# Moving the last group's routing pieces ahead among the first expert tiles, and narrowing the memsets between its row scatters

## The reference

```python
x = x + tanh(g_xattn) * xattn(ctx, layernorm(x), mask, mask, ...)
xn = layernorm(x)
scores = sigmoid(xn @ gate.T + bias)            # 2048 tokens x 9 experts
top_scores, selected = top_k(scores, 2)         # divided by their sum
for e in range(9):
    h = silu(xn @ w1[e].T) * (xn @ w3[e].T)     # hidden size 352
    out = out + cw[:, e:e+1] * (h @ w2[e].T)
x = x + tanh(g_ffn) * out
```

## Time and profile before

| what | us |
|---|---|
| median of 3 runs (lowest, highest) | 239.15 (238.38, 239.47) |
| the profiled execution's own time | 237.12 |
| its span in the trace | 235.3 |
| PE busy | 196.8 |
| DVE, ACT, POOL busy | 141.3, 142.6, 131.9 |

### The profile page before, as it was taken

The page is one execution under the profiler, slowest core; times in us unless marked ns, Lnnn a source line. Parts: engine busy times, 40 slices in busy tenths (PEclk is TensorE's granted clock), DMA queues, the critical chain, the costliest instruction groups (busy, mean ns, idle before and its releaser), DMA issues.

```text
span 235.3 us, 5763 instructions
## 1 busy us (share of the span) xinstructions
PE 196.8 (84%) x1527; PEld 156.2 (66%) x1528; DVE 141.3 (60%) x511; ACT 142.6 (61%) x400; POOL 131.9 (56%) x229
## 2 busy tenths in 40 slices
PE   8999986999999998997796799907999999999100
PEld 3676754666667665664685789807899999998100
DVE  1469996788997698887394794401344433443045
ACT  2287859988878786886258456602666666665100
POOL 4246844233325876776878587777555555655400
PEclk9999999999999999999799999985999999999855
DMA  6999999999300100011471321113221122160095
GB/s 182 352 380 250 405 382 363 400 326 292 117 4 13 37 23 23 25 35 38 101 225 38 91 51 55 45 34 98 64 67 43 54 54 61 46 215 27 0 329 206
DMA packets 19546, 32.65 MB, mean 139 GB/s; under 512 B 2609, under 2 KB 11830, under 8 KB 19394
## 3 DMA queue, kind: packets, MB, share of 16 engines
q1 hardware_dynamic: 16498, 27.18, 35.9%
q0 software_dynamic: 2304, 4.24, 5.5%
q10 hardware_dynamic: 720, 0.95, 1.4%
HBM read 15.77 MB, written 17.10 MB: 140 GB/s over the span
## 4 chain that ended last, share of the span: by engine, by line
PE 54%; DVE 16%; POOL 8%; issue 8%; ACT 8%; DMA 4%; SPq 0%; POOLq 0%; DVEq 0%; ACTq 0%
PE pt_ps L1230 9%; PE score_ps L1192 5%; PE score_ps L1194 4%; PE score_ps L1193 4%; PE pt_ps L1239 4%; PE score_ps L1050 4%; PE ps_a L1100 3%; POOL x_rows L564 3%; PE pt_ps L1088 3%; PE pt_ps L990 3%; ACT probs L385 3%; DVE xs L982 3%; PE score_ps L1000 2%; PE ps_b L1157 2%; POOL spare L550 2%
## 5 line engine op out<-in xcount | busy, mean ns | idle before, releaser
L582 POOL DMA_INDIRECT y_rows<-probsT,ids x40 | 39.6, 990 | 25.2 <-ACT probsT L453 17.2
L385 ACT ACTIVATE probs<-score_ps,less 128x128 f32<-128x128 f32 x128 | 37.8, 418 | 0.4 <-DVE less L773 0.4
L924 DVE TENSOR_TENSOR xg_low<-ps_a,xg_high 128x128 fp32r<-128x128 f32 x40 | 11.7, 292 | 43.5 <-ACT xg_high L438 26.8
L564 POOL DMA_INDIRECT x_rows<-stage,slot x32 | 32.5, 1017 | 8.0 <-POOL spare L550 4.5
L1230 PE MATMUL pt_ps<-w,probsT 128*128 x234 | 33.4, 280 | 2.1 <-ACT probsT L460 2.1
L1230 PEld LDWEIGHTS pt_ps<-w,probsT 128*128 128x128 f32 x234 | 31.3, 194 | 3.2 <-issue 2.9
L453 ACT ACTIVATE probsT<-pt_ps,xg 128x128 f32<-128x128 f32 x39 | 14.3, 367 | 30.0 <-PE pt_ps L1230 23.5
L1192 PE MATMUL score_ps<-w_high,xg_low 128*128 x80 | 30.3, 379 | 0.6 <-DVE probs L931 0.2
L931 DVE TENSOR_TENSOR probs<-probs,score_ps 128x352 f32<-128x352 f32 x40 | 20.8, 520 | 12.2 <-issue 6.1
L1193 PE MATMUL score_ps<-w_low,xg_high 128*128 x80 | 26.4, 330 | 0.0
L1194 PE MATMUL score_ps<-w_high,xg_high 128*128 x80 | 26.3, 328 | 0.0
(11 more groups left out here) (153 smaller groups left out, 427.6 us busy)
## 6 DMA issues: line engine op xcount, KB each, us to landing
x_rows<-pads SPq DMA_DIRECT2D x1, 9945.0 KB, 39.5
w_low<-in_w13T SPq DMA_DIRECT2D x3, 1056.0 KB, 10.8
xg<-x_rows SPq DMA_DIRECT2D x40, 65.0 KB
ctx_r<-in_ctxT SPq DMA_DIRECT2D x4, 512.0 KB, 7.2
w<-in_w2T SPq DMA_DIRECT2D x1, 1728.0 KB, 13.4
kheads<-y_rows SPq DMA_DIRECT2D x3, 512.0 KB, 5.0
mask_b<-in_mask SPq DMA_DIRECT2D x4, 256.0 KB, 7.9
out<-xs SPq DMA_DIRECT2D x1, 1024.0 KB
```

What stands on the lines that cost most here:

```text
L385: last = nc.scalar.activation(probs[:, r % 2, h, :], score_ps[:, r % 2, h, :], ACT.Exp, bias=less[:, r % 2, h:h + 1])
L564: pool.indirect_dma_start(x_rows[:, :], bass.IndirectOffsetOnAxis(ap=slot[:, par, c, p:p + 1], axis=0), stage[:, par, c, p, :], None, boun ...
L582: pool.indirect_dma_start(y_rows[:, :], bass.IndirectOffsetOnAxis(ap=ids[:, r:r + 1], axis=0), yt[:, r, :], None, bounds_check=last_row, o ...
```

## The change

The pieces that the last group needs before its rows can be scattered stand one to two tiles earlier, and some pieces change place with them:

- Batch 15's row transposes (`turn_rows(18)` on PE, `turned_back(18)` on ACT) go into tile 3: on PE behind the six products with w1 and w3 and ahead of the products with w2; on ACT behind the silu and ahead of the scaling.
- `gate_and_out(18)` on PE and the two table loads with the exponential on ACT go from behind tile 4 to behind tile 3.
- On DVE `table_counts(1)` goes from tile 2 to tile 0; logits and clamp from 4 to 3; `table_rows(1)` stays in 3 but behind them; `make_keys(3)` from 5 to 3; `choose(3)` from 6 to 4; weigh, ranks, places and labels from 7 to 5; `table_used(1)` and `table_counts(2)` from 8 to 6; `table_rows(2)` from 9 to 7. `rank(3)` on PE goes from 7 to 5.
- On POOL the scatters of the last group stand behind the y scatters of tiles 1, 1, 2 and 3 instead of 3, 4, 5 and 6. The memsets of the last group are 128x128 instead of 128x384 and the one behind each scatter is gone. Group 2 keeps its own.

```diff
@@ scalar: tile, between
+                if isinstance(k, int) and k == 3:
+                    turned_back(NB + 2)
...
                 if k == 3:
-                    turned_back(NB + 2)
-                if k == 4:
                     nc.scalar.preload_act_table(ACT.Exp)
                     sigmoid_exps(NG - 1)
                     nc.scalar.preload_act_table(ACT.Silu)
@@ gpsimd
-            def space():
+            def space(n):
-                nc.gpsimd.memset(spare[:], 0.0).then_inc(spaced, 1)
+                nc.gpsimd.memset(spare[:, 0:n], 0.0).then_inc(spaced, 1)
...
-                        space()
+                        space(3 * D if g < NG - 1 else D)
...
                 tile(k, k % TR)
-                if k in range(3, 3 + UN):
-                    scatter(NG - 1, k - 3)
-                    space()
+                for p in {1: (0, 1), 2: (2,), 3: (3,)}.get(k, ()):
+                    scatter(NG - 1, p)
@@ vector: between
                 if k == 0:
                     norm2(NB - 2)
                     table_used(0)
+                    table_counts(1)
                 if k == 1:
                     second(NB - 1)
                 if k == 2:
-                    table_counts(1)
                     norm2(NB - 1)
                 if k == 3:
-                    table_rows(1)
-                if k == 4:
                     logits_of(NG - 1)
                     clamp(NG - 1)
+                    table_rows(1)
+                    make_keys(NG - 1)
+                if k == 4:
+                    choose(NG - 1)
                 if k == 5:
-                    make_keys(NG - 1)
-                if k == 6:
-                    choose(NG - 1)
-                if k == 7:
                     weigh(NG - 1)
                     keep_ranks(NG - 1)
                     place_rows(NG - 1)
                     label_rows(NG - 1)
-                if k == 8:
+                if k == 6:
                     table_used(1)
                     table_counts(2)
-                if k == 9:
+                if k == 7:
                     table_rows(2)
@@ tensor: tile, between
+                if isinstance(k, int) and k == 3:
+                    turn_rows(NB + 2)
...
                 if k == 3:
-                    turn_rows(NB + 2)
-                if k == 4:
                     gate_and_out(NB + 2)
-                if k == 7:
+                if k == 5:
                     rank(NG - 1)
```

## The result

The changed kernel took 237.3 us (median of 20 runs, 235.27 to 239.56). The kernel before took 239.47 (20 runs, 237.57 to 240.4). The ratio is 0.9908, with a 95% interval of 0.9884 to 0.9931. The gain is 2.2 us where 10.8 were predicted, and the time lies outside the predicted range. The profiled execution took 237.52 with a span of 235.7; before, the two were 237.12 and 235.3.

A forecast was written before the change was run, and what follows sets the result against it. PE, busy 84% of the span, was taken to set the pace. Tile 16 starting 8.6 us earlier plus 2.2 from full clock made 10.8, so 239.15 us became 228.4, range 225.5 to 232.5.

The forecast's parts named there:

- PE's own arrival: PE's path through the early expert tiles to tile 16, forecast at 151.4 us, later than its data at 149.7.
- T(16): Start of PE's transpose of tile 16, other tiles likewise; forecast 8.6 us earlier, at 151.4 instead of 160.02.
- the 0.3 allowed for entering the loop: Allowance of 0.3 us added to seven even tiles, taking PE's transpose of tile 16 from 151.1 to 151.4.
- ACT's gap of 2.58: ACT's unexplained 2.58 us wait ahead of 134.24; might delay data to 151.6, no change to the sum.
- B: Rival: tile 16's data still come last, at 154.4; time 231.4 to 233.5 us; chance 0.13.
- C: Rival: DVE's routing pieces hold up PE's early tiles; 236.4 us in full, 231 if half; chance 0.12.
- costed at 0.2 each: DVE's 16 small operations from logits to keys, estimated at 3.2 us together, ending at 124.7.
- The row transfer of 1.42: POOL's time per last-group transfer with its narrowed memset, forecast at 1.42 us instead of 1.65.
- D: Rival: no measurable change, because the labels come when they did before; 239 us; chance 0.03.
- E: Rival: slower, as DVE's work holds up POOL's descriptor writing and stretches its transfers; 241.5 us; chance 0.02.
- theory S: Theory from the experiments, not the prediction: POOL's indirect transfers standing too close together make PE's releases reach ACT and DVE late.
- 2.2 for the clock: Tile 16 on PE, forecast 2.2 us shorter because without idle time ahead it runs at full clock.

The follow-up runs named there:

- r1: The changed kernel without any edit, run again on the fourth chip; 226.21 us, ratio 0.9525 to the kernel before.
- e8: The changed kernel with the last group's memsets 128x256 instead of 128x128; 227.83 us, ratio 0.9617.
- r3: The kernel before in its old order, with only the last group's memsets narrowed to 128x128 and none behind its scatters; 234.34 us, ratio 0.9845.
- e1 to e4: First chip: changed kernel with 128x384 last-group memsets; plus those behind scatters; old order, narrow memsets; first variant plus early y-scatter memsets: 236.76, 237.69, 237.87, 239.24 us.
- e5: The changed kernel with 128x384 last-group memsets and a 128x128 memset ahead of the y scatters of tiles 4 to 36; 227.27 us, then 227.2.

## Why the prediction went wrong, point by point

**The step that failed** is PE's own arrival: "From there on nothing stands between tiles: seven tiles at 2.06 to 2.07". On the chip of the result four of these tiles took 17.3 us where four at 2.07 take 8.3. That is 9.0 of the 11.8 by which T(16) missed its 151.4. In place of the even pace stood late releases of ACT and DVE and the low clock behind them. Of the rest, 3.0 was already there at T(9), 139.6 against 136.6. The two add up to some 0.3 too much, because the 0.3 allowed for entering the loop wasn't needed.

**Its sign was in the trace before.** ACT's gap of 2.58 has no named releaser either. The prediction put it at nothing in its sum and counted it once in rivals B and C. It wasn't the only one. DVE's timeline of the kernel before has another:

```profile
167.09 0.52 DVE L931 TENSOR_TENSOR probs<-probs,score_ps 128x352 f32<-128x352 f32 x1 [1.60 <-remote]
```

As one of a kind that can come back at every tile, it would have had to stand in the range as often as tiles lie open. The prediction leaned there on the Trainium skill (Runtime: NRT & Kernel Launch, Instruction fetch mechanics) for a gap at a place of the stream. The trace disagrees: r1 has the same streams and not one such gap, and in the late execution the longest came at one instruction, L456, of four tiles in a row.

**The 3.0 us up to T(9)** are partly DVE's. Its counts, logits, clamps and table rows were costed at 0.2 each. In the changed kernel on the chip of the result (DVE's timeline) some took 0.64 to 0.76:

```profile
115.66 0.68 DVE L874 TENSOR_SCALAR in_tiles<-placed 1x9 f32<-1x9 f32 x1
...
123.39 0.68 DVE L702 TENSOR_SCALAR logits<-z 128x36 f32<-128x36 f32 x1
...
125.13 0.64 DVE L894 TENSOR_SCALAR row_of<-row_f 1x8 int32<-1x8 f32 x1
...
126.91 0.76 DVE L713 TENSOR_SCALAR over<-sigs 128x36 f32<-128x36 f32 x1
```
```profile
115.35 0.97 POOL L565 DMA_INDIRECT x_rows<-stage,slot  x1 [0.28 <-POOL spare L551]
...
123.09 0.97 POOL L565 DMA_INDIRECT x_rows<-stage,slot  x1 [0.28 <-POOL spare L551]
...
124.76 0.97 POOL L565 DMA_INDIRECT x_rows<-stage,slot  x1 [0.28 <-POOL spare L551]
...
126.68 0.99 POOL L565 DMA_INDIRECT x_rows<-stage,slot  x1 [0.28 <-POOL spare L551]
```

The second fence is POOL's timeline. Each DVE operation ends within 0.04 us of the transfer that POOL is issuing: 115.66 + 0.68 is 116.34, and 115.35 + 0.97 is 116.32. In r1 the four took 0.57, 0.18, 0.16 and 0.30, 1.55 us less together, and from logits to keys DVE needed 3.2 there (122.34 to 125.52), as forecast. This isn't the mark of a late chip: in e8, with no late release, L702, L894 and L713 took 0.65, 0.63 and 0.76. Labels ended at 133.71 here, 131.13 in r1 (forecast 130.1).

**Point by point where nothing is late (r1)**, forecast ahead of measured: T(5) 125.3 and 126.34; POOL's first memset 130.8 and 131.76; T(9) 136.6 and 137.20; last row scatter 144.2 and 145.53; T(16) 151.4 and 152.36; T(17) behind it 2.1 and 2.11; no wait ahead of T(16); clock around it near 1 and 1.00. The row transfer of 1.42 is 1.47 (133.23 less 131.76, memset to memset). The times up to T(16) are 0.6 to 1.3 us late. T(39) comes at 201.02, before at 211.87: 10.85 sooner, where 10.8 was forecast. That the two agree so well is luck. T(16) came 7.66 sooner, not 8.6, and tile 16 gave 2.12. The remaining 1.07 came behind T(17), where the forecast had nothing (47.62 us from T(17) to T(39) before, 46.55 in r1): the trace of before has its second unnamed wait there. r3 prices the memsets alone: 3.2 us of the whole (237.55 less 234.34).

**The rivals.** B fell: none of the three traces of the changed kernel shows PE waiting for data at T(16). C named the right place, tile distances of 3 us and more, but not the releaser: DVE's pieces weren't it. D fell: the labels did come sooner, at 133.71 and 131.13 instead of 135.36. E said the opposite of what came: the last group's transfers kept their 0.97 to 1.00, and it was DVE whose operations grew longer beside POOL's. E's 241.5 doesn't follow from its own sum either: ten transfers longer by twice 1.15 would put T(16) 11.5 later still, near 252. What came had no rival of its own: the gap of the earlier trace rows, recurring.

**What stays open.** What differs where releases were late (in the runs of the result and on the first chip) isn't known. There the kernel before took 239.5 and 239.8, on the other four chips 236.3 to 237.6. The kernel before loses 2 to 3.5 us there, the changed kernel 11; their traces have two and nine unnamed waits of over 0.5 us.

Late releases are tied in time to POOL's transfers, and more closely than theory S asked. In the six traces with late releases (before, after, e1 to e4) ACT and DVE start 49 times behind a wait without a named releaser from 110 to 180 us. Each of these starts lies 0.62 to 0.82 or 1.33 to 1.51 us behind the start of one of POOL's indirect transfers, while starts behind named waits lie at any distance. Above, 145.30 is 0.71 and 146.01 is 1.42 behind 144.59. All waits of over 0.5 us among them stand in or just behind stretches of transfers at 1.50 or less; row transfers at 1.68 have none. In the other 14 traces no such wait occurs, with transfers as close as 1.27. So spacing seems to decide where releases are late on a chip that has them, and something else whether it has them. The test of the first half would be e5 on a late chip, and e5, run twice, never met one. Why releases come late, and whether some counter or queue is shared with POOL's transfers, no run shows.

**A better version?** None was found. Where nothing is late the changed kernel takes 226.2 and 226.7, its variants with the new order 226.4 to 227.8; none is below it by what the runs can tell. For a chip with late releases it stays open.

## What to carry to other kernels

An idle gap whose releaser has no name is a term of its own: look how often its kind could recur in the work that the change exposes, and keep that in the range. Before a difference of a few per cent is explained by the kernel, run the unchanged kernel on a second chip; four experiments on one chip agreed on a cause that four other chips didn't show. Where nothing else stood in the way, a stall taken away by moving work forward paid nearly what its rows said (7.66 of 8.6 us at T(16), 2.12 of 2.2 for the clock).

## What the runs showed of the hardware

**A release can be 2 us late on one chip and in time on the next.** PE's product ended at 139.35, and ACT, idle, started at 141.58. In this stretch ACT's late starts fell on steps of about 0.74 us (141.58, 142.31, 143.78, 146.01, 146.74, 148.23) and DVE's on the same steps (140.84, 145.30, 149.74), half of the 1.48 between POOL's transfers. In all six traces that have them, late starts keep to two places behind a transfer, 0.62 to 0.82 and 1.33 to 1.51 us. Late releases cost a kernel of 226.2 us another 11.

**A small DVE operation can last until POOL's transfer is over.** Here TENSOR_SCALAR operations of 8 to 36 columns, begun 0.23 to 0.37 us into a transfer, took 0.64 to 0.76 us and ended with POOL's 0.97. Not each overlap does it: in r1 L702 started at 122.57, 0.06 into such a transfer, and took 0.18. The Trainium skill (SBUF — State Buffer, Who interferes with whom) says that GpSimd and a DVE operation such as tensor_scalar or cast in a two-port mode lock each other out, and that the one that issues first holds the ports. The trace agrees with it for the four long ones, where POOL was first; L702 in r1 started behind POOL too and didn't wait.
